# Coefficient products in token halves, the router's hidden state ahead of the tanh, and a new order for the last two tiles

## The reference

```
x = x + tanh(g0) * attention(layernorm(x), ctx)                 # 16 heads of 16, causal, keys and values from ctx (64 wide)
n = layernorm(x)
h = silu(n @ W_up.T + b_up) @ W_down.T + b_down                 # hidden state, 128 wide
q = h @ W_q.T                                                   # router input; 8 heads x 2 sides x 64
sim = q . keys ; top 8 of 45 on each side ; top 8 of the 64 sums # 64 (head, k) slots for each token
z = silu((h . down_embed[e]) * softmax(score))                  # e = x * 45 + y, one expert for each slot
x = x + tanh(g1) * sum_slots z * up_embed[e]
```

## Time and profile before

| | before |
|---|---|
| median of 3 runs | 1220.84 us (1219.28 to 1221.39) |
| the profiled execution | 1225.47 us, of which its span is 1223.7 |
| busy in the span | PE 1143.9 us (93%), PE weight loads 1026.9, DVE 1036.6 (85%), ACT 765.2, POOL 332.4 |
| granted TensorE clock, mean | 0.978 |

### The profile page before, as it was taken

One profiled execution on the slowest core, in us unless ns is written; L12 is line 12 of the kernel. 1 busy time (PEld: TensorE's weight loads), 2 busy tenths in 40 slices (PEclk: granted clock), 3 DMA queues, 4 the chain that ended last, 5 costly groups with the idle time before them and its releaser, 6 DMA issues. The chain is left out here.

```text
span 1223.7 us, 47668 instructions
## 1 busy us (share of the span) xinstructions
PE 1143.9 (93%) x19004; PEld 1026.9 (84%) x19004; DVE 1036.6 (85%) x4238; ACT 765.2 (63%) x2602; POOL 332.4 (27%) x149
## 2 busy tenths in 40 slices
PE   6876999999999999999999999999999999999968
PEld 4765888888889888888988888888888898888857
DVE  3477889988888898888999888879889889988992
ACT  5656666667766666766666677656676766667411
POOL 4130333321233332123333122333212333320220
PEclk9987999999999999999999999999999999999988
DMA  8034655644554564456465445645445645643581
GB/s 221 11 100 117 151 104 130 151 119 121 134 151 99 134 150 117 112 144 125 108 151 138 120 116 149 145 88 151 124 114 135 151 110 124 150 123 104 142 188 28
DMA packets 304948, 154.53 MB, mean 126 GB/s; under 512 B 282735, under 2 KB 295895, under 8 KB 296535
## 3 DMA queue, kind: packets, MB, share of 16 engines
q1 hardware_dynamic: 304727, 151.47, 50.9%
HBM read 79.62 MB, written 4.72 MB: 69 GB/s over the span
## 5 line engine op out<-in xcount | busy, mean ns | idle before, releaser
L368 POOL TENSOR_TENSOR rstd<-veps,minus_half 128x1 f32<-128x1 f32 x32 | 67.9, 2123 | 713.6 <-DVE veps L851 713.6
L1203 PE MATMUL bank<-ue,coef 128*128 128x256 f32 x1024 | 233.9, 382 | 1.4 <-ACT coef L427 1.4
L1203 PEld LDWEIGHTS bank<-ue,coef 128*128 128x128 f32 x1024 | 191.6, 192 | 25.6 <-ACT coef L427 1.6
L948 PEld LDWEIGHTS bank<-z,hot_rT 128*128 128x128 bf16 x1984 | 150.4, 96 | 22.3 <-issue 22.3
L969 PEld LDWEIGHTS bank<-uc,hot_r 128*128 128x128 bf16 x5952 | 152.4, 96 | 15.2 <-issue 15.1
L969 PE MATMUL bank<-uc,hot_r 128*128 128x32 bf16 x5952 | 155.8, 176 | 9.3 <-issue 8.4
L1015 PEld LDWEIGHTS bank<-hT,deT 128*128 128x128 f32 x1024 | 128.3, 194 | 38.7 <-ACT hT L577 29.8
L948 PE MATMUL bank<-z,hot_rT 128*128 128x32 bf16 x1984 | 156.5, 177 | 1.0 <-DVE picked L643 1.0
L948 PE MATMUL bank<-zl,hot_rT 128*128 128x32 bf16 x1984 | 155.7, 177 | 0.8 <-issue 0.8
L948 PE MATMUL bank<-zll,hot_rT 128*128 128x32 bf16 x1984 | 155.7, 177 | 0.0
L1015 PE MATMUL bank<-hT,deT 128*128 128x128 f32 x1024 | 134.3, 280 | 22.7 <-ACT hT L577 22.7
(11 more groups left out here) (161 smaller groups left out, 2269.4 us busy)
## 6 DMA issues: line engine op xcount, KB each, us to landing
hot_rT<-expert_rows SPq DMA_DIRECT2D x62, 1024.0 KB, 6.3
xt<-in_x SPq DMA_DIRECT2D x32, 128.0 KB, 2.4
out<-x1k SPq DMA_DIRECT2D x32, 128.0 KB, 2.2
ct<-in_ctx SPq DMA_DIRECT2D x32, 64.0 KB, 2.2
ue<-in_L_ffn_up_embed SPq DMA_DIRECT2D x1, 2048.0 KB, 13.4
z<-in_L_ffn_W_up SPq DMA_DIRECT2D x1, 1024.0 KB, 7.9
expert_rows<-r_h SPq DMA_DIRECT2D x64, 8.0 KB, 1.8
WupT<-expert_rows SPq DMA_DIRECT2D x1, 1024.0 KB, 4.8
```

Source lines behind the costliest of these rows:

```text
L368: nc.gpsimd.tensor_tensor(rstd[:, :], veps[:, :], minus_half[:, :], ALU.pow).then_inc(S["rstd_ok"], 1)
L948: last = mm(bank[:, 32 * (q - 16 * k):32 * (q - 16 * k) + 32], (last_rT_parts if T.last else hot_rT_parts)[k // 2][:, q % (Q // 2), :], pa ...
L1203: last = mm(bG0[:, 0:DM], coef[:, c, :, :].rearrange("r h q -> r (h q)"), ue[:, c, :], start=(c == 0), stop=(c == C - 1))
```

## The change

1. `coef_parts` works on halves of the token pairs: twelve products of 64x512 in place of six of 64x1024, all three n of the first half before the second half. `scatter(0)` waits only for the first half (`uc0`), `scatter(2)` for the second (`uc1`). The semaphore `uc2` is gone.
2. ScalarE's order after `exps(1)` becomes `hT`, `zt`, `ex` in place of `ex`, `zt`, `hT`.
3. `gathered_sum(0)` moves ahead of `gathered(1)` on DVE.
4. For the last tile, GpSimd's zl and zll also wait for the tile's own `rh_ok` (end of its decoding) and for the `hotc` of the tile before.
5. In turn 34, DVE makes the router weights (`gates_of_slots`) ahead of u and the one-hot rows (`hot_T`) behind the coefficients, and PE does the scatters of tile 30 ahead of the gathers of tile 31.

```diff
--- before.py
+++ after.py
...
@@ -373,6 +373,9 @@
 
                     Fw.wait("z_sb3")
                     Fw.free2("g_pe3")
+                    if Fw.last:
+                        Fw.wait("rh_ok")
+                        B.wait("hotc")
                     Fw.wait("sums_ok")
                     if A:
                         A.wait("xn2_ok")
@@ -566,16 +569,16 @@
                     up_tanh(1)
                 if A:
                     exps(1)
-                if B and not B.last:
-                    expert_exp(B)
-                if Ct:
-                    Ct.wait("zp_ok")
-                    nc.scalar.activation(zt[:, :], zp[:, :], ACT.Tanh, scale=0.5).then_inc(S["zt_ok"], 1)
                 if Fw:
                     Fw.wait("hid_pe")
                     Fw.free("z_pe3")
                     nc.scalar.activation(hT[:, :], bD[:, 0:TILE], ACT.Identity, bias=bdn_sb[:, 0:1],
                                          scale=1.0 if Ct else 0.5).then_inc(S["hid_sb"], 1)
+                if Ct:
+                    Ct.wait("zp_ok")
+                    nc.scalar.activation(zt[:, :], zp[:, :], ACT.Tanh, scale=0.5).then_inc(S["zt_ok"], 1)
+                if B and not B.last:
+                    expert_exp(B)
                 if A:
                     probs_T(0)
                     probs_T(1)
@@ -655,16 +658,18 @@
                     B.wait_dma(f"rows_in{part}")
                     nc.vector.tensor_scalar(rT, rT, p_iota[:, 0:1], None, ALU.is_equal).then_inc(S[f"hotrT{part}"], 1)
 
-                def coef_parts(n):
+                def coef_parts(qh, n):
 
                     Ct.wait(f"uh{n + 1}")
-                    Ct.free("w_pe3")
+                    Ct.free("w_pe1" if qh == 0 else "w_pe3")
+                    qs = slice(qh * Q // 2, (qh + 1) * Q // 2)
                     for half in range(2):
                         rows = slice(64 * half, 64 * half + 64)
-                        last = nc.vector.tensor_tensor(uc[rows, n, :, C * half:C * half + C].rearrange("s q (c b) -> s q c b", b=2),
-                                                       hot_c[rows, :, :].rearrange("s q (c b) -> s q c b", b=2),
-                                                       u_h[rows, n, :, :].unsqueeze(2).to_broadcast([64, Q, C // 2, 2]), ALU.mult)
-                    last.then_inc(S[f"uc{n}"], 1)
+                        last = nc.vector.tensor_tensor(uc[rows, n, qs, C * half:C * half + C].rearrange("s q (c b) -> s q c b", b=2),
+                                                       hot_c[rows, qs, :].rearrange("s q (c b) -> s q c b", b=2),
+                                                       u_h[rows, n, qs, :].unsqueeze(2).to_broadcast([64, Q // 2, C // 2, 2]), ALU.mult)
+                    if n == 2:
+                        last.then_inc(S[f"uc{qh}"], 1)
 
                 def scores_max(half):
                     A.wait("s_pe")
@@ -761,7 +766,7 @@
                 if Ct:
                     Ct.wait("sm_ok")
                     if Ct.last:
-                        Ct.free("uc2")
+                        Ct.free("uc1")
                     nc.vector.tensor_tensor(
                         hot_c[:, :, :].rearrange("s q (c b) -> s q c b", b=2),
                         c_sm[:, cs, :, :].unsqueeze(2).to_broadcast([128, Q, C // 2, 2]),
@@ -782,11 +787,11 @@
                 if A and (Ct or not Fw):
                     scores_max(0)
                 if Ct:
+                    gathered_sum(0)
                     gathered(1)
                 if A and (Ct or not Fw):
                     scores_max(1)
                 if Ct:
-                    gathered_sum(0)
                     gathered(2)
                     gathered_sum(1)
                     gathered(3)
@@ -803,6 +808,8 @@
                     nc.vector.reciprocal(rinv[:, :], rsum[:, :]).then_inc(S["rinv_ok"], 1)
                 if A and not Fw:
                     copy_weights(dve, WDN[0])
+                if B and B.last:
+                    gates_of_slots()
                 if Ct:
 
                     Ct.wait("zt_ok")
@@ -817,13 +824,12 @@
                 if Ct:
                     Ct.wait("uh2")
                     nc.vector.tensor_tensor(u_h[:, 2, :, :], u_l[:, :].unsqueeze(2).to_broadcast([128, Q, 2]), u_h[:, 1, :, :], ALU.subtract).then_inc(S["uh3"], 1)
+                    for qh in range(2):
+                        for n in range(3):
+                            coef_parts(qh, n)
                     if B and B.last:
-                        gates_of_slots()
                         hot_T(0)
                         hot_T(1)
-                    coef_parts(0)
-                    coef_parts(1)
-                    coef_parts(2)
                 if A:
                     A.wait("rT_sb")
                     A.free("wo_pe")
@@ -951,9 +957,8 @@
 
                 def scatter(k):
 
-                    if k == 0:
-                        for n in range(3):
-                            Ct.wait(f"uc{n}")
+                    if k % 2 == 0:
+                        Ct.wait(f"uc{k // 2}")
                     Ct.wait_dma(f"hotr_in{k // 2}")
                     bank = (bS if Ct.last else bG)[k % 2]
                     if k >= 2:
@@ -1171,14 +1176,15 @@
                     dense(2)
                 if B and B.last:
                     slots_T()
-                    for k in range(4):
-                        gather(B, side, k)
                 if Ct:
                     scatter(0)
                     scatter(1)
                     scatter(2)
                 if Ct:
                     scatter(3)
+                if B and B.last:
+                    for k in range(4):
+                        gather(B, side, k)
                 if A and (Ct or not Fw):
                     output()
                 if A and not Fw:
```

More of the change, by code:

```diff
@@ L195, in flamingo_layer @@
             "rows_in0 rows_in1 hotrT0 hotrT1 hotr_in0 hotr_in1 hotc g_pe0 g_pe1 g_pe2 g_pe3 gm0 gm1 gm2 gm3 zs0 zs1 zs2 zs3 zp_ok zt_ok u_ok uh1 uh2 uh3 ul_ok "
-            "uc0 uc1 uc2 w_pe0 w_pe1 w_pe2 w_pe3 w_sb0 w_sb1 w_sb2 w_sb3 out_pe y_ok y_out0 y_out1"
+            "uc0 uc1 w_pe0 w_pe1 w_pe2 w_pe3 w_sb0 w_sb1 w_sb2 w_sb3 out_pe y_ok y_out0 y_out1"
         ).split()}
```

## The result

The changed kernel is slower: 1237.51 us median of 4 runs (1237.14 to 1237.87) against 1220.06 us (1218.51 to 1221.39). The ratio is 1.0143, 95% interval 1.0126 to 1.0161, so +17.4 us. The forecast was 1231, in a range of 1210 to 1241.

The account below looks back on a forecast made before the run. The prediction took the chain DVE topi, ScalarE, scores, DVE to close the turn at 35.64 us. Its terms, 17.7 - 5.8 - 1.8 = +10.1 us on 1220.84, gave 1230.9 us, 0.8% slower; range for 8 in 10: 1210 to 1241.

Parts of the forecast that it names:

- The bound: Steady turn: the chain DVE topi, ScalarE, scores, DVE closes the turn by itself at 35.64 us; PE has slack.
- hT ahead of zt and ex: ScalarE in a steady turn: PE gets dense(0) 0.89 us sooner, worth nothing on the chain; zt ends at 614.23.
- The sum: DVE in a steady turn: gathered_sum(0) fits in the 0.59 us wait; zp 0.55 us earlier, u gains 0.47 us.
- The halves: DVE's coefficients: twelve products take 5.3 us where six take 4.22, a loss of 1.08 us a turn.
- Rival 2: DVE's products: halves are cheap, fixed part 0.06 us instead of 0.17; turn -0.11 us, about 1210; chance 0.11.
- The turn: Turns 4 to 32: +0.61 us each, 35.64 becomes about 36.25; 29 turns, +17.7 us.
- What is absorbed: Tile 2 to tile 30: of 7.5 us lost in a few longer turns, 5.8 come back; bounds 3 and 7.5.
- The tail: Turns 33 to 35: -1.8 us in all, bounds -5.8 and +2.
- Rival 1: Steady turn: PE closes it, so hT's 0.89 us comes back each turn; 25 us, about 1196; chance 0.10.
- Rival 3: It cancels: products of 0.40 us (+0.77) and the full 7.5 us absorbed; about 1220; chance 0.10.
- Rival 4: More is lost: zt behind hT or GpSimd's late zl; another 0.3 us a turn, 1240 and above; chance 0.05.

Follow-up runs that it names:

- e10: The changed kernel with the 16 position searches of topi ahead of the 16 instructions of best and besti on VectorE; 1189.48 us, ratio 0.9749.
- e12: The kernel before with the position searches of topi first, nothing else; 1218.35 us, ratio 0.9991.
- e3: The kernel before with ScalarE's order hT, zt, ex, nothing else; 1223.47 us, ratio 1.0029.
- e11: The changed kernel with whole coefficient products and the position searches of topi first; 1203.82 us, ratio 0.9875.
- e5: The kernel before with gathered_sum(0) ahead of gathered(1), nothing else; 1207.11 us, ratio 0.9881.
- e2: The kernel before with the twelve half products and the scatter's waits by halves, nothing else; 1244.06 us, ratio 1.0198.
- e9: The changed kernel with ScalarE's old order (ex, zt, hT); 1227.69 us, ratio 1.0062.
- e4: The changed kernel with six added matmuls ahead of the scores, their results overwritten, to keep PE busy; 1232.26 us, ratio 1.0107.
- e6: The kernel before with points 4 and 5 alone (GpSimd's wait, turn 34's order); 1220.52 us, ratio 1.0002.

## Why the prediction was right or wrong

**The bound.** Right for the changed kernel. The chain from topi over ScalarE and the scores closes the turn: e10 moves topi and nothing else and takes 48 us from the changed kernel. Not complete: the prediction noticed that PE and ScalarE met within 0.1 us and read it as slack of PE. PE's own arrival hung on a second closed chain: in the kernel before over zt and hT, where moving topi alone gave 0.09 us a turn (e12), and with hT moved ahead over the products and the scatter (e3, e11). With the halves in place that did not change the forecast, since the first chain was then the longer one by 1 us.

**hT ahead of zt and ex.** Right that it gains nothing, and that u moves 0.47 us and not 0.55 us. Wrong in what else it does: see the clock.

**The sum.** Right, -0.56 us a turn by itself (e5), -0.47 behind hT.

**The halves.** The mechanism right, the size 0.1 us too large: 12 products took 5.20 us where 5.3 were forecast, +0.98 where 1.08 were. One of 64x512 takes 0.419 us:

```profile
L668 DVE TENSOR_TENSOR uc<-hot_c,u_h 64x512 bf16<-64x512 bf16 x384 | 161.0, 419 | 5.3
```

Two forms of the same instruction, 1024 elements 0.685 and 512 elements 0.419, give 0.153 us fixed. At the 0.96 GHz of the Trainium skill, "VectorE: DVE Perf Modes", section on the TRN2 errata, that is 147 cycles: the trace agrees with the about 150 of that section's text, and not with the 58 of its table. Rival 2, which went by the table, falls with it.

**The turn.** +0.51 us, 36.14, where +0.61 and 36.25 were forecast; 29 turns make 14.8 us, not 17.7.

**What is absorbed.** This step failed, in two ways. The prediction took 5.8 us of lost time back. The old lost time is nearly gone in three kernels in which PE idles ahead of the scores and no turn ran at the lower clock (0.1 us in e2 and e9, 0.5 in e4). But in the changed kernel new time is lost in its place, 7.1 us in nine turns at the lower clock, which the prediction did not have: between the two profiled executions -5.8 us should have read -0.6. And part of the old lost time was in the profiled execution only: it took 1225.47 us where the median is 1220.06, the profiled run of after 1237.87 against 1237.51. Carrying the 4.6 us over to both and taking back 5.8 us of loss counted some of the same microseconds twice. e6 has the turns of the kernel before and was profiled in an execution of 1219.39 us: it lost 2.1 us. Beside such an execution the changed kernel loses 5 us more.

The two profiled spans differ by 12.4 us (1236.1 - 1223.7): +13.7 in the 28 turns (14.3 of length, -0.6 of lost time), +1.1 ahead of hT of tile 2, -2.4 behind hT of tile 30. The remaining 5 us to the medians' +17.4 are the profiled execution of before. The forecast had the direction and the largest term by the mechanism; that 1231 came within 6.5 us was partly luck, since the turn term was 2.9 us too high (17.7 for 14.8) and hid as much of what this step missed.

**The tail.** Right in the steps named for VectorE. Behind hT, zt and so u come late in turn 33; ab_i is free; and zp, one multiplication of 128x64, is blocked while GpSimd runs zl and zll:

```profile
1166.39 0.22 DVE L816 SCALAR_TENSOR_TENSOR u<-zt,zp 128x64 f32<-128x64 f32 x1 [1.45 <-ACT zt L579]
...
1183.98 0.17 DVE L733 TENSOR_SCALAR ab_i<-besti 128x64 uint32<-128x64 uint32 x1
...
1194.46 2.18 DVE L801 TENSOR_TENSOR zp<-zs,p_sm 128x64 f32<-128x64 f32 x1
```

```profile
1192.96 3.60 POOL L386 TENSOR_TENSOR zll<-zl 128x2048 bf16<-128x2048 f32 x1
```

GpSimd ends at 1196.56, zp at 1196.64. GpSimd's new wait gave back 2.91 us at ab_i (3.08 became 0.17), where 3.0 was forecast, and took 1.95 us at zp (0.23 became 2.18), where +1.7 was. The row of zp agrees with the exclusive lock of the Trainium skill, "SBUF — State Buffer", section "SBUF: two separate sides", for an instruction with two SBUF inputs; ab_i has one input, so its row in the kernel before bears only on the section's other case, a two-port mode, and that it ran in one is not shown.

From hT of tile 30 to the end the changed kernel takes 104.1 us and the one before 106.5, so -2.4. That stretch also holds the half products of turn 32 (+0.98), so the last three turns by themselves gave -3.4, where -1.8 was forecast. The difference lies behind zp, in the scatters, the gathers and PE's stalls there: the end of zp in turn 34 is 43.9 us from the end before and 39.5 after, -4.4 where +0.2 and -2.9 were forecast. Whether that is the new order is not shown: the same distance from hT of tile 30 is 107.1 us in e6 and 107.2 in e9, which have it too, and e6 as a whole gains nothing.

**The rivals.** Rival 1 is refuted by e3, rival 2 by the products' duration. Rival 3 needed both a cheaper product and all losses absorbed. Rival 4, more is lost, had the right direction and not its cause: in turns 4 to 32 neither zt nor GpSimd, but the clock.

## What to carry to other kernels

A wait of the busiest engine is worth its time only if no other chain closes the turn at the same length. Add up the candidate chains, once around, from rows: here two of them came to the turn's length within 0.1 us. Relieving one alone did nothing (e12 for topi, e3 for hT), while e10, which relieves both (topi first, and hT and the scatter early), is 18 us faster than the moved sum alone (1189.48 against 1207.11). And before cutting an instruction into halves to let a consumer start early, put its fixed cost (0.15 us here, six times a turn) on the engine's own chain: the same halves cost 30 us or gained 14, by whether that engine's last result had been moved forward.

Compare a profiled execution's own time with the median before counting its disturbances as something that a change can win.

## What was not expected of the hardware

The sum of PE's idle time does not decide on the clock. In 28 turns the changed kernel has 33 us of it and nine turns at the lower clock; e2 has 42 us, e9 27 us, and neither has one. The stretch of e2:

```profile
113.00:1137.00 1024.00, 981.71 (x16548) 880.14 (x16548) 923.07 (x3864) 663.99 (x2267) 286.19 (x112) 1.00 0.51 127
```

PE's waits in 26 to 28 of the turns (total us, times, longest us), first in the changed kernel, then in e9, then in e2:

```profile
PE bank L1003 <- ACT up_act L437: 16.3, 28, 0.6
PE bank L1003 <- issue: 15.7, 27, 0.7
```

```profile
PE bank L1003 <- ACT up_act L437: 15.8, 27, 0.6
PE bank L1020 <- ACT hT L580: 5.4, 27, 0.4
PE bank L1003 <- issue: 4.5, 23, 0.3
```

```profile
PE bank L1016 <- ACT hT L577: 19.9, 26, 1.0
PE bank L999 <- ACT up_act L434: 15.7, 27, 0.6
PE bank L999 <- issue: 4.7, 25, 0.3
```

In the changed kernel nearly all of it stands in two waits close together around the first matmuls of the scores, 0.6 us each. In e2 and e9 the second is the same, the first is 0.2 us, and the rest stands at hT. Filling that one place (e4) removed the stretches, so the waits there are needed for them. Whether it is their length, their sum or their closeness that counts was not tested, and why nine of 28 turns are hit and the others not stays open.
